# Attention rewritten: one ring of PSUM banks, two-bank exponentials, attention sums two key blocks at a time, no transposes of the output

## What is computed

```python
x = x + layernorm(attention(layernorm(x)))
x = x + layernorm(moe(layernorm(x)))

latent = x @ Wc_down                        # 256 -> 128
q = (latent @ Wq_up).reshape(B, T, 16, 16)  # 16 heads of 16
kv = latent @ Wkv_up                        # one key and one value for all heads
att = where(causal, q @ k.T / 4, -inf)
y = softmax(att) @ v
out = y @ Wc_proj

assign = argmax(x @ centroids.T)            # each token to one of 8 experts
out = x + relu(affine_layernorm(x) @ W1[e] + b1[e]) @ W2[e] + b2[e]
```

## Time and profile before

| | |
|---|---|
| median of three runs | 1029.45 us |
| profiled execution, its span | 1031.02 us, 1029.3 us |
| layernorm and latent | 0 to 39 us |
| attention: keys and queries made, maxima of two groups | 39 to 98 us |
| attention: 16 groups | 98 to 599.5 us |
| routing | 599.5 to 717 us |
| experts | 717 to 1029 us |
| busy: PE, DVE, ACT, POOL | 916, 712, 589, 243 us |
| granted TensorE clock, mean | 0.923 |

### The profile page before, as it was taken

How to read it: one execution, slowest core, us unless ns; L and a number is a source line. 1 busy time by engine, 2 the same in 40 slices (tenths; PEclk the granted TensorE clock), 3 DMA queues, 4 the chain that set the end, 5 groups by cost and what they waited for, 6 DMA issues and landing times. The chain is left out here.

```text
span 1029.3 us, 24227 instructions
## 1 busy us (share of the span) xinstructions
PE 915.8 (89%) x5774; PEld 537.1 (52%) x5775; DVE 711.6 (69%) x2533; ACT 588.6 (57%) x1281; POOL 243.2 (24%) x386
## 2 busy tenths in 40 slices
PE   5799999979999999999999868972699999999994
PEld 3312333323333333333333247771699999999993
DVE  6499888868888878888883017766466666666652
ACT  3601776657767576676777845530355656565661
POOL 1200212202222112211111213320334343433311
PEclk9955999999999989999999988865799999999998
DMA  9421111011111111111100025660100100011000
GB/s 341 177 52 41 26 39 35 22 26 23 33 31 24 28 29 28 28 26 27 33 2 2 1 93 154 219 202 31 50 31 31 31 31 30 28 36 33 17 16 6
DMA packets 43408, 54.31 MB, mean 53 GB/s; under 512 B 11406, under 2 KB 32550, under 8 KB 43184
## 3 DMA queue, kind: packets, MB, share of 16 engines
q1 hardware_dynamic: 39568, 44.80, 15.1%
q0 software_dynamic: 3744, 8.40, 2.6%
HBM read 31.92 MB, written 9.31 MB: 40 GB/s over the span
## 5 line engine op out<-in xcount | busy, mean ns | idle before, releaser
L586 ACT ACTIVATE PR<-ST 128x512 f32<-128x512 f32 (+2 forms) x640 | 310.0, 561 | 170.1 <-PE ST L507 169.3
L650 DVE CUSTOM_DVE_ANT_0 junk<-SM,causal 128x512 bf16<-128x512 f32 (+3 forms) x512 | 222.9, 486 | 50.0 <-PE SM L457 45.8
L507 PE MATMUL ST<-Q,KC 99*128 99x512 bf16 (+3 forms) x768 | 230.3, 335 | 14.5 <-issue 8.1
L653 DVE TENSOR_REDUCE MP<-SM 128x1 f32<-128x512 f32 x256 | 166.2, 680 | 22.2 <-PE SM L457 21.8
L484 PE MATMUL OB<-PR,VC 128*32 128x512 f32 (+3 forms) x1536 | 166.4, 498 | 1.7 <-ACT OS L576 0.9
L793 POOL TENSOR_SCALAR_AFFINE_SELECT PR<-PR 128x512 f32<-128x512 f32 x128 | 81.2, 634 | 342.3 <-ACT PR L586 342.3
L507 PEld LDWEIGHTS ST<-Q,KC 99*128 99x128 bf16 x768 | 69.0, 99 | 175.3 <-ACT PR L586 110.0
L1484 PE MATMUL hp<-XNT,WS 128*128 128x128 f32 x1248 | 148.1, 278 | 2.4 <-DVE XNT L1556 2.4
L1484 PEld LDWEIGHTS hp<-XNT,WS 128*128 128x128 f32 x1248 | 147.6, 195 | 4.9 <-DVE XNT L1556 3.1
L1492 PE MATMUL yp<-W2s,HT 128*128 x624 | 141.3, 380 | 0.7 <-DVE z L1568 0.7
L457 PE MATMUL SM<-KN,Q 96*128 96x512 bf16 (+3 forms) x384 | 125.5, 373 | 12.2 <-DMA Q<-T 5.6
(11 more groups left out here) (178 smaller groups left out, 911.9 us busy)
## 6 DMA issues: line engine op xcount, KB each, us to landing
Q<-T SPq DMA_DIRECT2D x384, 32.0 KB, 2.0
W1s<-in_L_ffn_W_dram SPq DMA_DIRECT2D x8, 1024.0 KB, 16.4
W2s<-in_L_ffn_W_dram SPq DMA_DIRECT2D x8, 1024.0 KB, 7.3
Y<-in_L_attn_x_dram SPq DMA_DIRECT2D x8, 512.0 KB, 6.5
XQ<-in_L_attn_x_dram SPq DMA_DIRECT2D x8, 512.0 KB, 3.6
x_rows<-XQ SPq DMA_DIRECT2D x8, 512.0 KB, 7.8
b2s<-in_L_ffn_b_dram SPq DMA_DIRECT2D x1, 1024.0 KB, 4.9
KN<-K SPq DMA_DIRECT2D x24, 32.0 KB, 2.0
```

The lines of the kernel that those rows point to most:

```text
L507: last = pe.matmul(ST[u % RB][:, at:at + NQ - off], KC[0:KR, j * P:(j + 1) * P], Q[0:KR, g * GH + h, c * NQ + off:(c + 1) * NQ], start=Tru ...
L586: act.activation(PR[s % RB][:, heads[0]:heads[-1] + 1, off:NQ], ST[u % RB][:, 0:len(heads) * (NQ - off)].rearrange("p (h q) -> p h q", h=l ...
L650: op = dve.tensor_tensor_reduce(junk[:, n % 2, at:at + w], src, causal[:, NQ - w:NQ], 1.0, LOWEST, ALU.add, ALU.max, dst)
L653: op = dve.tensor_reduce(dst, src, AX, ALU.max)
```

## The change

- **PSUM.** `ST` becomes two double banks of 2 x 512. Everything else except the sums shares one ring of three banks (`ring`, `RING = 3`): maxima, the transposes of the maxima, query and key pieces, and values, in one fixed list of events (`EVENTS`) that PE and DVE both follow. Event k waits until DVE is done with event k-3.
- **Exponentials.** Two heads of 512 or 384 columns, or four of 256 or 128, go through one activation: 20 a group in place of 40.
- **Lead of the maxima.** `schedule` puts 22 banks of maxima (`EARLY`) ahead of the first scores, catches up in steps 0 to 3 of group 0, and from there keeps 38 banks ahead (`LEAD`), which is one group and two banks. The last group has no maxima beside it.
- **Sums.** `pv` takes two steps at a time, after every odd step, two to three steps late; the ring `PR` has four buffers.
- **Output.** Each value row of `V` is followed by a row of ones, so `OB` holds numerators in even rows and each denominator 16 times in odd rows. SP sends the two from `OS` by DMA to `YT`, which is kept with features on partitions, and to `DEN` (`send_out`). Once for every two groups and each half of the queries DVE inverts `DEN`, 128 x 512, in place (`inverse`), and POOL multiplies (`normalise`). The four PE transposes a half, L694 and L700 go.
- **Maxima's split.** The five small operations on the maxima are now POOL's (`split_max`, twice a group on 16 columns); DVE keeps one `merge`.
- **Pieces.** The first copy of a piece from PSUM is DVE's, no longer ACT's. Values are projected straight, 8 matmuls, without transposes.
- **Sequences.** Keys and values have two buffers each (`K[b % 2]`, `V[b % 2]`), and the loops are written out, without a drain between sequences.
- **Queries' DMAs.** A group's queries go in 12 DMAs of 64 KB, not 24 of 32 KB. At the start SP sends all 48 before the first group's maxima.
- **Memory.** The W1 weights of experts 6 and 7 load only in the routing stage; until then their space holds a `PR` buffer, `OS` and `DEN`.
- **Routing.** `ys`, `turn_y` and `yt` go, since `YT` is there already.

```diff
-UNITS = [[(h,) for h in range(GH)] if NQ - off > NQ // 2 else [(h, h + 1) for h in range(0, GH, 2)]
-         for _, _, off in STEPS]
...
+UNITS = [[(h, h + 1) for h in range(0, GH, 2)] if NQ - off > NQ // 2 else [tuple(range(GH))] for _, _, off in STEPS]
...
-LAG = 2
-RB = 3
+RB = 4
+RING = 3
...
+LEAD = 38
+EARLY = 22
+MLAT = 5
...
+    def reached(x):
+        return EARLY + x * (c0 + LEAD - EARLY) / c0 if x < c0 else x + LEAD
...
-        ST = [psum(f"ST{k}", [P, NQ]) for k in range(RB)]
-        SM = [psum(f"SM{k}", [P, NQ]) for k in range(RB)]
+        PR = [sb(f"PR{k}", [P, GH, NQ]) for k in range(RB - 1)]
+        late = [W1s[:, c, LATE * F:E * F].rearrange("p (h q) -> p h q", h=GH) for c in range(DC)]
+        PR.append(late[0])
...
+            def event(k):
+                kind, a, b = EVENTS[k]
+                if k >= RING:
+                    pe.wait_ge(ring_done, DONE_AT[k - RING])
...
+                bank = ring[k % RING]
...
+            def scores(n, s, u):
...
+                t = NU * n + u
+                if t >= 2:
...
+            def pv(pair):
+
+                for t in (2 * pair, 2 * pair + 1):
+                    n, s = divmod(t, len(STEPS))
+                    c, j, off = STEPS[s]
                     pe.wait_ge(exp_done, NU * n + UNIT_AT[s + 1])
...
+                    if s in DIAG:
+                        pe.wait_ge(masked, len(DIAG) * n + DIAG.index(s) + 1)
...
+                    for h in range(GH):
+                        last = pe.matmul(OB[32 * h:32 * h + 32, off:NQ], V[n // NG % 2][:, j, :, :].rearrange("p d u -> p (d u)"),
+                                         PR[t % RB][:, h, off:NQ], start=j == 0, stop=s in (C0, LAST))
...
+            for n in range(NB):
+                for s in range(len(STEPS)):
+                    for u in range(UNIT_AT[s], UNIT_AT[s + 1]):
+                        scores(n, s, u)
+                        for k in range(EVENT_AT[NU * n + u], EVENT_AT[NU * n + u + 1]):
+                            event(k)
+                    t = len(STEPS) * n + s
+                    if t % 2 and t > 2:
+                        pv((t - 3) // 2)
...
+            def out_copy(n, c):
+                act.wait_ge(pv_done, (len(STEPS) * n + (LAST if c else C0)) // 2 + 1)
+                past(act, o_out[c], 32 * n)
+                act.activation(OS[c], OB[:, :], ACT.Copy).then_inc(o_copied, 1)
...
+            def piece(k, b, name):
+                parts_sent(dve, b, name)
+                dve.tensor_copy(parts(name)[0], ring[k % RING][0:rows_of(name), :]).then_inc(part1, 1)
...
-            def out_norm(b, g, c, k, stage):
-
-                o = misc[:, :].rearrange("p (t h d) -> p t h d", t=NQ // P, h=GH)
-                if stage == 0:
-                    dve.wait_ge(misc_ready, k + 1)
-                    dve.wait_ge(misc_free, k)
-                    dve.reciprocal(rden[:, :, :], o[:, :, :, HD]).then_inc(o_step, 1)
-                else:
-                    dve.wait_ge(o_step, QC * (b * NG + g) + c + 1)
-                    y = Y[:, ds((b * TB + c * (NQ // P)) * D, (NQ // P) * D)]\
-                        .rearrange("p (t h d) -> p t h d", t=NQ // P, d=HD)[:, :, g * GH:(g + 1) * GH, :]
-                    rb = rden[:, :, :].rearrange("p t (h u) -> p t h u", u=1).broadcast_to([P, NQ // P, GH, HD])
-                    dve.tensor_tensor(y, o[:, :, :, 0:HD], rb, ALU.mult).then_inc(misc_free, 1)
-
...
+            def inverse(n, c):
+                dve.wait_ge(o_out[c], 32 * (n + 1))
+                dve.reciprocal(DEN[c], DEN[c]).then_inc(inverted, 1)
...
+                n0, n1, n2 = (NMX[c][:, a, :] for a in range(3))
+                top = mx[:, :] if c else MP[r % 2][:, 0, :]
+                then(pool.tensor_scalar(n0, top, -1.0, None, ALU.mult))
+                then(pool.tensor_tensor(mr[:, 0, :], top, n0, ALU.add))
+                then(pool.tensor_scalar(n1, mr[:, 0, :], -1.0, None, ALU.mult))
+                then(pool.tensor_tensor(mr[:, 1, :], mr[:, 0, :], n1, ALU.add))
+                pool.tensor_scalar(n2, mr[:, 1, :], -1.0, None, ALU.mult).then_inc(nmx_ready, 1)
...
+            def normalise(n, c):
+
+                b, g = divmod(n, NG)
+                pool.wait_ge(inverted, n // 2 * QC + c + 1)
+                y = YT[:, g // 2, b * T + c * NQ:b * T + (c + 1) * NQ]
+                pool.tensor_tensor(y, y, DEN[c], ALU.mult).then_inc(normed, 1)
...
+                for r, part in enumerate(QPART):
+                    made(b, f"q{half}1", part)
+                    for c in range(QC):
+                        sp.dma_start(Q[r * HD:(r + 1) * HD, g, c, :, :].rearrange("d h q -> d (h q)"),
+                                     (T1, T2, T3)[part][rows, half, c * NQ:(c + 1) * NQ]).then_inc(q_in[g], 16)
...
+            def send_out(n, c):
...
+                rows = slice(g % 2 * GH * HD, (g % 2 + 1) * GH * HD)
+                y = YT[rows, g // 2, b * T + c * NQ:b * T + (c + 1) * NQ]
+                sp.dma_start(y, OS[c][0:P:2, :]).then_inc(o_out[c], 16)
+                sp.dma_start(DEN[c][rows, :], OS[c][1:P:2, :]).then_inc(o_out[c], 16)
...
             send_keys(0)
-            for g in range(2):
+            for g in range(NG):
                 send_queries(0, g)
-            send_max(0, 0)
-            for g in range(2, NG):
-                send_queries(0, g)
-            loops(sp, group)
-
-
-def route(nc, spare, x, Wc_proj, centroids, params, ident, eps, Y, W2s, w2_v, w2_in, x1_rows, IDX, EX, PT):
+            sends(0, EVENT_AT[0])
+            for n in range(NB):
+                b, g = divmod(n, NG)
...
-                def turn_y(t, c):
-
-                    pe.wait_ge(ys_ready, t + 1)
-                    past(pe, yt_copied, DC * t + c)
-                    for i in range(QT):
-                        last = pe.transpose(ytp[:, i * P:(i + 1) * P], YS[:, i, c * P:(c + 1) * P], ident[:, :])
-                    last.then_inc(yt_ready, 1)
-
...
-                def ys(t):
-                    past(act, yt_ready, DC * t)
-                    act.activation(YS[:, :, :].rearrange("p t d -> p (t d)"), Y[:, ds(t * (QT * D), QT * D)],
-                                   ACT.Copy).then_inc(ys_ready, 1)
-
-                def yt(t, c):
-                    act.wait_ge(yt_ready, DC * t + c + 1)
-                    past(act, pj_ready, t)
-                    act.activation(YT[:, c, :], ytp[:, :], ACT.Copy).then_inc(yt_copied, 1)
```

More of the change, by code:

```diff
@@ new lines, with unit_of, max_units @@
+RING = 3
+def unit_of(bank, s):
+    w = NQ - STEPS[s][2]
+    if w > NQ // 2:
+        return bank[:, :, 0:w]
+    return bank.rearrange("p u q -> p (u q)")[:, 0:GH * w].rearrange("p (h q) -> p h q", h=GH)
+BW = NQ // P
+MS = GH * BW
+def max_units(c):
+    rows = [(h, i) for h in range(GH) for i in range(c * BW, (c + 1) * BW)]
+    whole = [(h, i, k, NQ, (k + 1) * BW == i + 1) for h, i in rows for k in range((i + 1) // BW)]
+    rests = [(h, i, (i + 1) // BW, (i + 1) % BW * P, True) for h, i in rows if (i + 1) % BW]
+    pairs = []
+    while rests:
+        one = rests.pop(0)
+        mate = next(k for k, two in enumerate(rests) if two[3] == NQ - one[3])
+        pairs.append([one, rests.pop(mate)])
+    return [[m] for m in whole] + pairs
@@ L97, in beyond @@
+EVENTS, EVENT_AT = schedule()
+DONE = []
+for event in range(len(EVENTS)):
+    if EVENTS[event][0] != "piece":
+        DONE.append(event)
+    if event and EVENTS[event - 1][0] == "piece":
+        DONE.append(event - 1)
+DONE_AT = [DONE.index(event) + 1 for event in range(len(EVENTS))]
 def beyond(t, start):
@@ new lines, in weights, with piece, values @@
+            def weights(name):
+                if name[0] == "k":
+                    return Wkv[:, 0:HD]
+                half = 2 * int(name[1])
+                return WqT[:, half:half + 2, :, :].rearrange("p g d h -> p (g d h)")
+            def piece(b, name, bank):
+                c = int(name[-1])
+                return pe.matmul(bank, weights(name), LT[:, b * T + c * NQ:b * T + (c + 1) * NQ], start=True, stop=True)
+            def values(b, bank):
+                for j in range(TB):
+                    last = pe.matmul(bank[:, j * HD:(j + 1) * HD], LT[:, b * T + j * P:b * T + (j + 1) * P],
+                                     Wkv[:, HD:2 * HD], start=True, stop=True)
+                return last
@@ L609, in _ @@
+            out_copy(NB - 1, 1)
         @block.vector
         def _(dve):
[L611 to L625 removed]
```

764 lines of the change are left out of this document (314 added, 450 removed), and 4 rows, old and new, of the table MISC.

## The result

The changed kernel takes **1069.69 us** (median of four runs, 1067.77 to 1070.56), the kernel before 1029.71 us in the same series. The ratio is 1.0399, with a 95% interval of 1.0366 to 1.0432. It is 4% slower. The forecast was 1039 us with a range of 995 to 1060, so its direction was right and its size was not, and the range did not hold the time.

A forecast was written before the change was run, and what follows sets the result against it. PE paced full steps, DVE 12% behind. Attention: 80 + 11 + 15 x 32.8 + 25 + 8.6 = 616.6 us, 17 later; routing gains 8: 1031.0 + 17 - 8 = 1040, median 1039, range 995 to 1060.

The forecast's parts named there:

- A group beside maxima: 32.8 us: Attention group with maxima running: DVE's maxima, stalls, reciprocals, merge, pieces and values sum to 32.8 us, against 30.6 before.
- Net: 2.1 us a group: Reciprocals of 512 denominator columns on DVE: 3.4 us each, partly hidden beside PE's sums, leaving 2.1 us a group.
- The clock stays at 0.50: Rival: PE stays at half clock in attention, a group takes some 42 us, the whole over 1150; chance 0.03.
- The sums two steps at a time: Paired sums on PE with a ring of three banks: DVE stands idle behind them, 5.4 us a group.
- PE's own need is 26.5 us, so it doesn't set the pace: PE's work in a group beside maxima, with sums and pieces: 26.5 us, below the group's 32.8.
- The start: Before attention's steady groups: scores start at 80 us, not 98.0; half clock and 16 more banks of maxima add 11.
- End and routing: After the last copy of the sums: 8.6 us to routing, which then gains 8 us.
- Boundaries: Between sequences: double buffers of keys and values remove the drain, worth 2.4 us a group.
- copies of the sums 32 to 34 us apart, without a longer one between sequences: Sign expected in the changed profile: evenly spaced groups in attention, with no longer gap where a sequence ends.
- The covered stall: Rival: DVE never idles behind paired sums; a group takes 28.7 us, the whole 978, half covered 1008; chance 0.30.
- The dearer reciprocal: Rival: DVE's reciprocal costs 8.3 ns a column, 0.9 us more each: 1054, with small waits 1050 to 1062; chance 0.10.
- the sum over p: DVE's idle time behind each of six sums a group, p - 0.67 us for PE's sum length p: 5.4 us altogether.

The follow-up runs named there:

- run 1025: Changed kernel with each reciprocal of the denominators over 16 of its 512 columns, all else kept: 1025.2 us, ratio 0.9971.
- the first fillers: Changed kernel with sixteen more matmuls of 512 columns, results unread, on PE in step 6 of every even group but the first: 1075.1 us.

## Why the prediction was wrong, by its own steps

Two windows carry most of this, 14 groups of the changed kernel and the same 14 with reciprocals of 16 columns:

```profile
112.42:592.37 479.95, 416.64 (x2796) 162.70 (x2796) 398.50 (x1210) 274.95 (x326) 137.58 (x282) 0.96 0.12 38
...
112.38:557.24 444.86, 399.96 (x2800) 160.26 (x2800) 359.71 (x1213) 273.69 (x327) 139.40 (x283) 1.00 0.12 41
```

- **"A group beside maxima: 32.8 us"** is the step that failed: measured 34.3. Fourteen groups make 21 of the 28 us by which attention ended late (routing from 644.9, forecast 616.6). Its parts: DVE's own work was right (22.7 + 3.4 + 0.8 + 1.5 + 0.3 = 28.7 forecast; 398.5 / 14 = 28.5 measured). Its idle time was not: 5.4 less the 1.3 hidden under reciprocals forecast, 5.8 measured. Two terms share the 1.5 us of error.
- **"Net: 2.1 us a group"** for the reciprocals is the first of them, and the one whose mechanism was incomplete. For the 3.1 of 3.35 us that the 16 columns leave out it gives 1.9 us a group; the two windows give 2.5, or 2.8 for each reciprocal. The half that stands beside a long sum was right (1.0 forecast, 0.8 in five of seven groups). The other half cost 4.5 where I had 3.2, because I looked only at DVE's time. PE was stopped for 2.2 to 4.1 us, in four of the groups with pieces once more for 1.5, and then ran at half clock. Fillers that keep PE busy in these waits gave back 13 us. That I still had 35 of the 44.5 us is partly luck: I had put all 35 down to DVE's time, and the reciprocals in four parts, with 6 us more of DVE's time, cost only 19.4.
- **"The clock stays at 0.50"** had a chance of 0.03, as a state for all of attention. That it falls for 3.4 to 6.8 us behind a stop of PE was not among the rivals, though the trace of the kernel before shows it behind two of its drains. This is the case I left out.
- **"The sums two steps at a time" was called the term that decides: 5.4 us a group.** The level was near: without whole reciprocals DVE is idle 6.1 us a group, 0.7 more than forecast. With 0.1 more of DVE's work this is the second part of the error, 0.8 us a group. The cause was wrong. I set it against an order of single sums "with an idle time of nearly nothing", and single sums leave 4.9 us. My own rows had said so: in the earlier trace rows DVE is busy 26.1 of 30.6 us with single sums, idle 4.5. Pairing costs 0.9 us in a group without pieces and whole reciprocals (30.20 less 29.33), 7 us in the kernel, and 2 as the change has it, which can't be told from nothing. It explains little of the 40 us.
- **"PE's own need is 26.5 us, so it doesn't set the pace."** The profile shows PE busy for 27.8 of 29.3 us with 16 columns and single sums. That figure is modelled, so it does not show what PE needs at least. That most of DVE's idle time still ends on PE says that PE takes part in setting the pace; how much of the 27.8 is work, and how much waits inside it, stays open.
- **The start.** Scores began at 80.90, forecast 80: right. But I charged 11 us against 18 gained and kept 7, and the first copy did not move. These 7 us are the third part of the miss. The clock stayed at half until 104, with one break of 3.4 us (until 102 before), and 34 banks of maxima are taken between the first scores and the first copy, where there were 17.5. Sending the first maxima earlier gained 7.
- **End and routing.** 9.2 us from the last copy to the start of routing (8.6 forecast), and 9 us gained behind it (8 forecast). Right.
- **Boundaries.** The sign "copies of the sums 32 to 34 us apart, without a longer one between sequences" did not come: they are 31.0 to 38.3 apart, and the first groups of the last three sequences take the longest (37.8, 38.3 and 36.7 us, for groups 4, 8 and 12). That there is no drain is right: with reciprocals of 16 columns group 12, which starts a sequence and has no pieces, takes 30.5 us. The pieces cost 1.6 us in each of the groups that have them (32.0 on average for groups 0 to 11 against 30.4, with 16 columns); I had 1.8 with the values.
- **Rivals.** The covered stall (0.30) did not come: DVE is busy 83% of a group. The dearer reciprocal (0.10) gave the nearest time, 1050 to 1062, but for another reason: its 3.35 us were as the rows had it.

The miss of 31 us adds up like this. Reciprocals that cost 44.5 us where the sum had 35 are 9.5. With 16 columns the prediction's own sum gives 1039 - 35 = 1004 and the run 1025, with no half clock in its groups. Of these 21 us, 7 are the start, 12 are fourteen groups that are 0.8 us too long each, and 2 are the rest. What stays open is why DVE idles for these 0.7 us a group more than the sum over p has it: its waits are of 0.2 to 1.8 us, most of them ended by PE, and no experiment priced them one by one.

## What to carry to other kernels

Price a long instruction not only by its own time but by what it stops elsewhere, and for how long: here 3.35 us in one piece cost 2.8 us on average and up to 6.2, and in four parts 1.2 on average ((1044.6 - 1025.2) / 16, the last two still whole). Before you blame one term for a wait, work out from the same rows how much of that wait the old order has; here it was 4.5 of 6.1 us. And look for copies: a value that stands sixteen times was cheaper to gather, invert once and spread by DMA (8% busy in that group) than to invert sixteen times: 1013.9 us against 1025.4 in four parts, the rest of the edits being the same.

## What the runs showed of the hardware

- Seven times PE's granted clock fell from 1.00 to 0.50 behind an idle time of PE of 2.2 to 4.1 us in a stream that was otherwise full, and stayed there for 3.4 or 6.8 us. Matmuls into a free bank that nobody reads, 5 to 17 at a time, cut the half clock between 105 and 590 us from 38 to 10 us and made the kernel 13 us faster. The Trainium skill, "TensorE: Matmul & The Clock Gate", Part 1, says that the array runs at 1.2 GHz when it has not been busy; the trace agrees (0.50 at 529 to 533 us, behind 4.08 us of idle time).
- A stop of PE did not decide it alone. With the first fillers the clock stayed at 1.00 behind two stops of 2.2 and 3.0 us, and with the reciprocals in parts it fell five times though PE never stopped for more than 1.5 us.
- A reciprocal of 128 x 512 takes 3.35 us on DVE, 6.5 ns a column, one of 128 columns 0.95 us, so four parts take 0.44 us more than one piece. A power of 128 x 512 on POOL takes 82 us.
